# Low parts of the weighted one-hots on ScalarE, and two loads behind the loop issued earlier

## The reference

```python
h = relu(layernorm(x))
msg = h[dst] @ W_i + h[src] @ W_j + edge_attr @ W_e
agg = segment_sum(edge_weight[:, None] * msg, dst)
x = x + agg + h @ W_self
h = relu(layernorm(x))
# twice, with W1 and W2: mean over the edges of each destination, then two products
mean = segment_sum(h[src], dst) / max(count, 1)
h = mean @ W_l.T + b_l + h @ W_r.T        # relu between the two
x = x + log_softmax(h)
```

## Time and profile before

| | us |
|---|---|
| median of 3 runs | 1671.7 (1670.32 to 1675.69) |
| the profiled execution, its own time | 1664.25 |
| its span, first to last instruction | 1662.4 |
| busy: TensorE / VectorE / GpSimd / ScalarE | 1418.8 / 979.4 / 727.2 / 600.4 |
| mean granted clock of TensorE | 0.933 of 2.4 GHz |

### The profile page before, as it was taken

The page is one execution under the profiler, slowest core; times in us unless marked ns, Lnnn a source line. Parts: engine busy times, 40 slices in busy tenths (PEclk is TensorE's granted clock), DMA queues, the critical chain, the costliest instruction groups (busy, mean ns, idle before and its releaser), DMA issues. The chain is left out here.

```text
span 1662.4 us, 25953 instructions
## 1 busy us (share of the span) xinstructions
PE 1418.8 (85%) x8448; PEld 1013.4 (61%) x8449; DVE 979.4 (59%) x4423; ACT 600.4 (36%) x1479; POOL 727.2 (44%) x783
## 2 busy tenths in 40 slices
PE   2587778898897887978898867799999979999997
PEld 0465556666675665766666546466666656666664
DVE  7799999889897987988897848200101030010204
ACT  5366656555646446465542325200000010020203
POOL 8777765667776766677677748000000000000000
PEclk9699889999998898999999988899999989999999
DMA  8467777988988978888799872577767657777773
GB/s 267 150 219 275 274 250 257 323 283 302 307 285 275 315 254 291 284 301 296 259 321 292 263 240 88 225 281 271 295 263 302 262 202 274 278 303 269 309 273 138
DMA packets 178853, 441.26 MB, mean 265 GB/s; under 512 B 24619, under 2 KB 104924, under 8 KB 175388
## 3 DMA queue, kind: packets, MB, share of 16 engines
q1 hardware_dynamic: 155996, 391.75, 65.3%
q0 software_dynamic: 22432, 46.97, 10.3%
q10 hardware_dynamic: 288, 0.85, 0.1%
HBM read 318.94 MB, written 120.55 MB: 264 GB/s over the span
## 5 line engine op out<-in xcount | busy, mean ns | idle before, releaser
L629 POOL DMA_INDIRECT home<-h_table,src_i x676 | 654.2, 968 | 280.3 <-issue 198.7
L1119 PE MATMUL psAE<-home 128*128 128x350 f16 x3528 | 541.3, 314 | 13.4 <-issue 8.7
L1119 PEld LDWEIGHTS psAE<-home 128*128 128x128 f16 x3528 | 339.1, 96 | 210.5 <-issue 12.6
L1029 PE MATMUL psAE<-home 128*128 128x256 f32 x1352 | 331.6, 406 | 44.1 <-DMA home<-h_table,src_i 20.1
L1029 PEld LDWEIGHTS psAE<-home 128*128 128x128 f32 x1352 | 274.0, 205 | 100.9 <-issue 54.7
L1477 DVE TENSOR_SCALAR home<-iota_h,dst_rel,home 128x128 f32<-128x128 f16 x832 | 222.6, 364 | 30.3 <-PE psAE L1029 27.8
L788 ACT ACTIVATE home<-psW 128x490 f16<-128x490 f32 x418 | 211.3, 577 | 59.1 <-PE psW L1038 47.4
L1419 DVE TENSOR_SCALAR home<-iota_h,tile 128x245 f16<-128x245 f16 x1004 | 208.9, 301 | 30.1 <-PE psW L1048 16.4
L1423 DVE TENSOR_SCALAR home<-iota_h,tile 128x128 f16<-128x128 f16 x1004 | 179.3, 281 | 0.0
L1581 DVE SCALAR_TENSOR_TENSOR home<-psAE,home 128x350 f32<-128x350 f32 x18 | 9.4, 523 | 253.6 <-PE psAE L1119 253.6
L1038 PE MATMUL psW<-home 128*128 128x245 f16 x836 | 127.8, 285 | 36.1 <-DVE home L1423 33.8
(11 more groups left out here) (211 smaller groups left out, 1173.6 us busy)
## 6 DMA issues: line engine op xcount, KB each, us to landing
home<-counts SPq DMA_DIRECT2D x36, 4287.5 KB, 13.7
counts<-home SPq DMA_DIRECT2D x126, 612.5 KB
home<-edges SPq DMA_DIRECT2D x64, 845.0 KB
weighted<-home SPq DMA_DIRECT2D x24, 1225.0 KB, 6.8
home<-weighted SPq DMA_DIRECT2D x36, 800.0 KB
home<-h_table,src_i POOLq DMA_INDIRECT x676
home<-h_table SPq DMA_DIRECT2D x36, 256.0 KB
home<-inv_row SPq DMA_DIRECT2D x36, 175.0 KB, 13.5
```

The lines of the kernel that those rows point to most:

```text
L629: pool.indirect_dma_start(out=rows[to][:, j, :], out_offset=None, in_=from_table[:, :], in_offset=bass.IndirectOffsetOnAxis(ap=src_i[b][:, ...
L1029: done = nc.tensor.matmul(psA[:, 0:2 * P].rearrange("p (n f) -> p n f", n=2), onehot[:, j, :], both_of(s, b, j), start=(j == 0), stop=(j = ...
L1119: last = nc.tensor.matmul((psA, psE)[r][:, 0:SNODES].rearrange("p (c d) -> p c d", c=SUPER), halves[:, a, n, :], tiles[:, :, a, :], start= ...
```

## The change

1. `weigh_hots` makes both parts of each weighted one-hot on ScalarE: eight activations a group in place of four, in the order high, low for each of the four node groups. `low_hots` on VectorE goes, with its five calls per dense chunk and its semaphore `whot_low`, for which TensorE waited in `weigh_pair`.
2. SP issues the load of the node weights ahead of the own rows' loads; the two waits for the stores of the node rows go with it, ahead of the waits for the own rows' stores and the dense pieces.
3. SP issues the second load of counts of the first pass as soon as the last mixing product is done, before it waits for the inverses; it was issued behind them.

```diff
@@ SP, behind the loop
             with sp.If(fast):
+                for b in range(2):
+                    sp.wait_ge(node_out[b], 16 * (CHUNKS // 2 - b))
+                sp.dma_start(node_weight_rows, node_rows[0, 0:USED].rearrange("(t p) -> t p", p=P)).then_inc(weight_in, 16)
                 sp.wait_ge(own_out, 16 * BLOCKS)
                 sp.wait_ge(piece_done, DSUPERS * PIECES)
                 for n, (lo, hi) in enumerate(OWN_PARTS):
                     columns = slice(lo * UNROLL * FEATS, hi * UNROLL * FEATS)
                     sp.dma_start(accN[:, columns], own_rows[:, columns]).then_inc(own_back[n], 16)
-                for b in range(2):
-                    sp.wait_ge(node_out[b], 16 * (CHUNKS // 2 - b))
-                sp.dma_start(node_weight_rows, node_rows[0, 0:USED].rearrange("(t p) -> t p", p=P)).then_inc(weight_in, 16)
...
                 sp.wait_ge(added[0], ADDED)
                 load_counts(1, 0)
+                sp.wait_ge(mixed[0], BLOCKS)
+                load_counts(1, 1)
                 sp.wait_ge(inv_made, 2)
                 sp.dma_start(inv_row.rearrange("(p n) -> p n", p=LINES), deg_lines).then_inc(inv_out, 16)
                 sp.wait_ge(inv_out, 16)
                 for p in PASSES:
                     if p == 1:
-                        sp.wait_ge(mixed[0], BLOCKS)
                         load_inverse(1, 0)
-                        load_counts(1, 1)
                         load_inverse(1, 1)
@@ ScalarE, weigh_hots
                 for j in range(4):
                     t, at = divmod(c * GROUPS + 4 * k + j, P)
-                    done = nc.scalar.activation(whot_all[k % 2][:, j, 0, :], ghot(4 * k + j)[1], ACT.Copy, scale=w_parts[t][:, 0, at:at + 1])
+                    for n in range(2):
+                        done = nc.scalar.activation(whot_all[k % 2][:, j, n, :], ghot(4 * k + j)[1], ACT.Copy, scale=w_parts[t][:, n, at:at + 1])
@@ TensorE, weigh_pair
                 pe.wait_ge(whot_ready, ORDER[i] * 5 + k + 1)
-                pe.wait_ge(whot_low, ORDER[i] * 5 + k + 1)
@@ VectorE
-                        if i and ORDER[i - 1] < DENSE:
-                            low_hots(i - 1, (4,))
...
-            def low_hots(i, ks):
...
-                        last = nc.vector.tensor_scalar(whot_all[k % 2][:, j, 1, :], iota_h[:, 0:P], tile_of(t)[:, 2, at:at + 1],
-                                                       w_parts[t][:, 1, at:at + 1], ALU.is_equal, ALU.mult)
-                    last.then_inc(whot_low, 1)
...
-                if c < DENSE:
-                    low_hots(i, (0, 1))
...
                 add_sums(i, c, base)
-                if c < DENSE:
-                    low_hots(i, (2, 3))
```

More of the change, by code:

```diff
@@ L238, in gnn_program @@
         own_hT = carve(accN, in_N, P)
+        assert in_N[0] <= USED
         node_weight_rows = accN[0:BLOCKS, USED:USED + P]
@@ L325, in gnn_program @@
         made, kept = sem("made"), sem("kept")
-        whot_ready, whot_low = sem("whot_ready"), sem("whot_low")
+        whot_ready = sem("whot_ready")
         w_out = [sem(f"w_out{h}") for h in range(2)]
```

## The result

The changed kernel takes 1687.7 us (median of 20 runs), the kernel before 1673.6 (20 runs): ratio 1.0075, 95% interval [1.0053, 1.0097], which is 12.6 us slower (8.9 to 16.2; the two medians are 14.1 apart) where 14.6 were forecast. The forecast time was 1686.3 us, its range 1673 to 1702.

What follows compares the result with a forecast made beforehand. The prediction took the chain through the chunks, not VectorE's busy time, to bound the loop. Loop +29.7 us (25.1 exposed ScalarE work, 4.6 clock) and tail -15.1 make +14.6 on 1671.7: 1686.3 us, range 1673 to 1702.

Steps and rivals of the forecast that it cites:

- What bounds the loop: Chunk loop: the chain through the chunks is last, GpSimd's gathers follow it; its standing grows some 25 to 30 us.
- The queue of 18.9 us: Eight dense chunks: ScalarE's work from first group to VectorE's second half, without idle, takes 18.9 us; loss 20.4 us.
- Only group 4 exposed in the four others: Four dense chunks with a late transfer: other groups hidden or nearly, group 4 costs 4 x 1.17 = 4.7 us.
- The clock's 4.6 us: Dense chunks: TensorE's longer gap before W4 brings its lower clock, 12 x 0.38 = 4.6 us, bounds 0 to 9.1.
- The loop in all: Chunk loop: exposed ScalarE work 25.1 us and clock 4.6 make +29.7 us, bounds 14.0 to about 44.
- The node weights, -5.9: Behind the loop: weights land first, GpSimd starts multiplying when the own rows' first part lands, 5.9 us sooner.
- The second counts, -9.2: Behind the loop: TensorE's 7.7 us gap before the second sum goes, and about 1.5 us of low clock.
- A: Rival, chunk loop: GpSimd's standing absorbs the delay, only the tail's gain is left, 1656.6 us; chance 0.12.
- its stronger form: Rival, chunk loop: VectorE is on the chain and all 57.5 us return, 1599 us; chance 0.04.
- C: Rival, chunk loop: the swap costs only the engines' busy-time difference, +18.5 us, giving 1675 us; chance 0.08.
- D: Rival, behind the loop: the early counts load collides, 7.7 and 1.5 us stay, +23.8, 1695.5 us; chance 0.08.
- B: Rival, chunk loop: TensorE's low clock reaches W4 and the sums everywhere, 44.1 us less 15.1, 1700.7 us; chance 0.13.

Runs made afterwards that it cites:

- e_counts: Kernel before with only the second counts load earlier; executed once, time not read; loop's last addition to end 662.7 us against 673.1.
- e_tail: Kernel before with only the two earlier loads (node weights, second counts), low parts still on VectorE; ratio 0.9919, 13.5 us less.
- e_weights: Kernel before with only the node weights' load earlier; executed once, time not read; loop's last addition to end 668.1 us against 673.1.
- e_swap: Kernel before with only the low parts moved to ScalarE, loads where they were; ratio 1.0157, 26.2 us more.
- e_ahead: e_tail with ScalarE making the high parts of group 4 ahead of the copy of W2; ratio 0.9855, 1643.0 us.
- e_nolow: e_tail with no low parts made by any engine, their buffers zeroed once and still multiplied by TensorE; ratio 0.9914.
- e_g4: e_tail with the low parts of group 4 alone on ScalarE; ratio 1.0018, 16.5 us over e_tail.

## Why the prediction was right, point by point

- **What bounds the loop** ("a delay of that chain reaches the loop's end in full"): right. The loop's last addition is 41.8 us later in the profiled run, GpSimd's standing 40.5 us longer (77.3 to 117.8). I had written 25 to 30; the two profiles differ by more than the medians do. The last addition comes at 989.3, 995.9, 1000.4 and 1004.7 us in the four profiles with the loop of before (`before`, `e_counts`, `e_tail`, `e_weights`) and at 1031.0 and 1034.1 in the two with the swap (`after`, `e_swap`); GpSimd stands 77 to 92 us in the four, 118 and 126 in the two, and 65 in `e_ahead`.
- **The queue of 18.9 us**: right in the two chunks where nothing else interfered (the first and the fifth), with 18.7 us. In the other six of the eight it is 19.7 to 21.6: in chunks 2 to 4 by the clock, in 6, 7 and 11 because a piece's transfer came late there too, which I had not counted. So one of my signs of being wrong did show: behind chunks 2, 3 and 4 ScalarE idles 2.1, 0.7 and 2.2 us before the sums' copy. It waited there for sums at the low clock, and the idle came on top of the queue and hid none of it. The working has a small slip: 8 x 18.9 less 131.1 is 20.1, not 20.4.
- **Only group 4 exposed in the four others**: right, 11.2 to 11.5 us from the sums to the second half instead of 10.0; from the first group on, the four take 5.6 us more together, forecast 4.7.
- **VectorE gives nothing back**: right, shown by `e_nolow`.
- **The clock's 4.6 us**: the order of size is right, the place is wrong. I had put it at W4; in the profile of after, W4 took 1.00 us in nine places and 1.13 to 1.30 in three. It fell on the sums of the early chunks, which I had kept as an upper bound only, and on W0 and W1: distances over 11.2 sum to 5.6 us, and three chunks lose 0.8 each at W1, about 8 in all. Where it falls is not fixed: in `e_g4` it was W4, 1.80 us in three places.
- **The loop in all**: +29.7 forecast; `e_swap` 26.2, interval 20.4 to 32.1. That is nearer than the parts are. From the first group to the second half the twelve chunks take 213.5 us before and 250.5 after, 37 more (and 252.7 in `e_swap` against 219.3 in `e_tail`, 33 more). The late pieces and the clock took more than I gave them, and it is not shown where the runs, with 26, get part of it back.
- **The node weights, -5.9**: -5.0 in one execution, but the step "GpSimd starts when the part lands" was not what set it. GpSimd started 11.3 us behind the own rows' issue, not 6: in the run of after the last sums ended 9 us behind that issue and were the last to come, and it started 1.1 us behind the last addition. In all nine traces with this load earlier it starts 1.1 us behind that addition, and 5.7 to 11.3 us behind the own rows' issue. TensorE's transpose of the weights stands behind the last sums' own transposes. What is shown is that the weights were no longer late.
- **The second counts, -9.2**: -10.4, and the idle gone in every kernel that has the load earlier.
- **Rivals**: A and its stronger form are excluded by `e_swap` and `e_nolow`; C (18.5 us in the loop) lies a little below `e_swap`'s interval (from 20.4), and a price per engine does not explain `e_g4`; D is excluded by `e_counts`; B was the right effect at less than half of its 19 us.

## What to carry to other kernels

An engine that is busy 86% of a stage may still be off the chain: before work is moved from it, look at what it waits for, and at the order of the queue that the work is moved to, where each added instruction delays all that stand behind it. Lay the receiving engine's queue end to end from measured spacings; here that gave 18.9 us for a measured 18.7 in the chunks that nothing else disturbed. The same queue shows what to turn instead: one copy behind four small instructions, rather than ahead, was worth 10.7 us, nearly as much as the two loads together (13.5).

## What the runs showed of the hardware that was not expected

Four activations of 128 elements hold ScalarE for 1.17 us when something follows and eight for 2.33 (320.89 to 323.22), though each is listed with 0.39 us: they overlap, so the price is 0.29 each. The length of one gap did not tell whether TensorE's clock falls to 1.2 GHz. Behind a gap of 2.49 us, eight matmuls took 1.00 us in the changed kernel (276.92) and 1.80 in `e_g4` (128.28, granted clock 0.50), both after more than 9 us of unbroken matmuls. Behind gaps of 1.4 to 1.5 us that followed a longer one they took 1.82 (259.72 and 262.98), and the sums after them 7.93.
